# Regrouping the attention output through memory before normalising it, and a final projection in two fp32r products

## The reference, cut to what matters

```python
# xattn: softmax over 4096 keys, for every batch, head and query row
dot = einsum('bhsd,bhtd->bhst', Q, K) / 4
out = einsum('bhst,bhtd->bhsd', softmax(dot), V)
out = out.reshape(B, T_src, D_MODEL)     # [b,h,s,d] read as rows of 256, WITHOUT a transpose back
x = x + out @ Wh.T + bh
x = x + linear_attention(layernorm(x))   # features exp(..), causal A, ctx / max(den, 1e-6), @ Wout
x = x + ffn(layernorm(x))                # (silu(x@wg.T) * (x@wu.T)) @ wd.T, integer weights / 127
```

## Time and profile before

| | |
|---|---|
| median of three runs | 877.13 us |
| the profiled execution, whole | 875.48 us |
| its span, first to last instruction | 873.8 us |
| mean granted TensorE clock | 0.990 |
| main loop's last value product ends at | 796.9 us of the span |
| the last batch's tail, with nothing beside it | 796.9 to 873.8 us |

### The profile page before, as it was taken

The page is one execution under the profiler, slowest core; times in us unless marked ns, Lnnn a source line. Parts: engine busy times, 40 slices in busy tenths (PEclk is TensorE's granted clock), DMA queues, the critical chain, the costliest instruction groups (busy, mean ns, idle before and its releaser), DMA issues.

```text
span 873.8 us, 20543 instructions
## 1 busy us (share of the span) xinstructions
PE 829.1 (95%) x8817; PEld 569.8 (65%) x8817; DVE 417.2 (48%) x746; ACT 541.5 (62%) x598; POOL 47.1 (5%) x76
## 2 busy tenths in 40 slices
PE   6899999999999998999999998999999999989876
PEld 5666666666666666676666665667666666657656
DVE  7433236444644445534654446354474444402654
ACT  2478887776577665667567764575657666672141
POOL 1034000000000000000000000000000000000010
PEclk9899999999999999999999999999999999999999
DMA  7486654646344333346343441443614333202000
GB/s 248 172 258 237 241 183 166 209 158 193 122 146 146 142 125 133 122 133 191 136 146 145 146 142 53 158 158 129 195 65 170 122 122 119 100 2 50 0 2 15
DMA packets 58768, 120.08 MB, mean 137 GB/s; under 512 B 21552, under 2 KB 29744, under 8 KB 55152
## 3 DMA queue, kind: packets, MB, share of 16 engines
q1 hardware_dynamic: 56880, 114.31, 38.3%
q0 software_dynamic: 1792, 4.40, 1.7%
HBM read 78.84 MB, written 37.75 MB: 133 GB/s over the span
## 4 chain that ended last, share of the span: by engine, by line
PE 82%; DVE 8%; issue 4%; DMA 2%; ACT 2%; DVEq 1%; POOL 1%; SPq 0%; POOLq 0%; ACTq 0%
PE ps_o L816 26%; PE ps_s L828 18%; PE ps_pa L662 10%; PE ps_pa L617 10%; PE ps_pa L763 2%; PE ps_pa L692 2%; PE ps_pa L788 2%; PE ps_pa L775 2%; PE ps_pa L754 1%; ACT probs L1258 1%; PE ps_pa L740 1%; DMA oscr<-y 1%; PE ps_pa L684 1%; PE ps_pa L795 1%; PE ps_pa L767 1%
## 5 line engine op out<-in xcount | busy, mean ns | idle before, releaser
L1258 ACT ACTIVATE probs<-ps_s 128x1024 f32<-128x1024 f32 x512 | 496.8, 1023 | 234.2 <-PE ps_s L828 227.7
L816 PE MATMUL ps_o<-probs,values 128*17 128x256 f32 x4096 | 256.1, 385 | 0.0
L828 PEld LDWEIGHTS ps_s<-qstack,kstack 64*128 64x128 f32 x2048 | 140.0, 186 | 99.6 <-ACT probs L1258 48.8
L828 PE MATMUL ps_s<-qstack,kstack 64*128 64x256 f32 x2048 | 194.0, 307 | 5.3 <-ACT probs L1258 5.3
L816 PEld LDWEIGHTS ps_o<-probs,values 128*17 128x17 f32 x4096 | 104.1, 98 | 98.7 <-issue 9.8
L1343 DVE TENSOR_SCALAR kparts<-ps_pa,b_heads 128x512 fp32r<-128x512 f32 x64 | 48.0, 750 | 107.4 <-PE ps_pa L617 107.1
L662 PE MATMUL ps_pa<-wv_hi,ctx_hi 128*128 128x256 f32 x256 | 79.6, 311 | 2.9 <-DVE wv_lo L1331 2.2
L1360 DVE TENSOR_TENSOR values<-ps_pa,bv_pair 128x512 f32<-128x512 f32 x64 | 44.2, 690 | 77.5 <-PE ps_pa L662 77.1
L662 PE MATMUL ps_pa<-wv_lo,ctx_hi 128*128 128x256 f32 x256 | 72.5, 283 | 0.0
L662 PE MATMUL ps_pa<-wv_hi,ctx_lo 128*128 128x256 f32 x256 | 72.4, 283 | 0.0
L617 PE MATMUL ps_pa<-ctx_hi,wk_hi 128*128 128x512 f32 x128 | 56.4, 441 | 0.0
(11 more groups left out here) (274 smaller groups left out, 786.7 us busy)
## 6 DMA issues: line engine op xcount, KB each, us to landing
kstack<-kscr SPq DMA_DIRECT2D x96, 512.0 KB, 5.3
kscr<-kparts SPq DMA_DIRECT2D x64, 512.0 KB, 2.7
ctx_raw<-ctxT SPq DMA_DIRECT2D x32, 512.0 KB, 6.5
qstack<-qscr SPq DMA_DIRECT2D x12, 256.0 KB, 3.5
qscr<-qparts SPq DMA_DIRECT2D x4, 512.0 KB, 3.1
xh<-x SPq DMA_DIRECT2D x4, 256.0 KB, 5.4
kstack<-kstack SPq DMA_DIRECT2D x2, 512.0 KB, 6.0
qstack<-ksample SPq DMA_DIRECT2D x4, 256.0 KB, 3.6
```

The lines of the kernel that those rows point to most:

```text
L816: last = mm(ps_o[32 * j:32 * j + DH + 1, g * S:(g + 1) * S], values[par][:, i, head_of_step(g, j), :], prob[:, j * S:(j + 1) * S], start=b ...
L828: last = mm(ps_s[s % 2][:, j * S:(j + 1) * S], kstack[par][rows, u, i * P:(i + 1) * P], queries[rows, u, :], start=True, stop=True)
L1258: nc.scalar.activation(probs[n % AHEAD][:, :], ps_s[n % 2][:, :], ACT.Exp, scale=float(DH) ** -0.5).then_inc(fast["exp_done"], 1)
```

## The change

1. **Loop, output's way.** `oT0` and `oT1` are gone. After `o`, SyncE writes `o_sb` as it is (heads on partitions, not normalised, denominators and unused rows too) to `oscr` in four DMAs of 32 partitions, pieces of 1 KB, 512 KB in all. Then it reads it back in two DMAs whose pieces are 64 B, to `o_rows`, which lies in the buffer `feat`: 128 rows x 17 x 16 for each half. A new VectorE stage `on` at step 9 waits for that read, takes all reciprocals in one instruction, checks all denominators at once, and scales with one instruction for each half into `y`. `yT` at 12 now waits for VectorE, not for a DMA.
2. **Loop, norms.** The addition of the `wh` and `wout` products is a stage by itself and the layernorm behind it another one, `ln1`, `ln2`, at the same step.
3. **Weights of the down projection.** They are loaded as integers to `qk` and `y` in two DMAs and cast once, at set-up, to an fp32r array `wd_r`. The loop multiplies by the same array read as fp32.
4. **The end, output's way.** As in 1; two of the four writes are issued by SyncE and two by ScalarE. The transposes of `o_sb` go, 34 `warm` products stand in one place where 12 and 26 stood, the denominator check stands behind the copy of `yT0`, and the verdict behind the first layernorm.
5. **The end, down.** VectorE cuts each `hid[:, k, :]` in a high and a low fp32r part (two more instructions and two waits for its own pipe for each k), and TensorE makes two fp32r products for each k and half, where one full fp32 product stood.

```diff
-AT = {"o": 1, "oT0": 3, "oT1": 4, "yT": 12, "wh": 13, "ln1T": 19, ...
+AT = {"o": 1, "on": 9, "yT": 12, "wh": 13, "ln1": 13, "ln1T": 19, ...
...
-        oscr = scratch("oscr", [H, S, DH], FP32)
+        oscr = scratch("oscr", [ST, 2 * DH, HALF, S], FP32)
+        o_rows = feat_flat[:, 0:ST * (DH + 1) * DH].rearrange("p (t d u) -> p t d u", t=ST, d=DH + 1)
...
+        def write_heads(eng, c, j):
+            t, e = j // CI, j % CI
+            eng.dma_start(oscr[t].rearrange("d (g e) s -> e d g s", e=CI)[e],
+                          o_sb[32 * j:32 * j + 2 * DH, :, :]).then_inc(c["o_written"], 16)
...
             def write_output(c, clock):
-                wait_all((c["operand"], c.at("operand", clock, "oT1")))
+                wait_all((c["operand"], c.at("operand", clock, "o")))
+                for j in range(GH):
+                    write_heads(sp, c, j)
+            def read_rows(t, landed):
+                sp.dma_start(o_rows[:, t, :, :], oscr[t, 0:DH + 1].rearrange("d h (a u) -> (h a) d u", u=DH)).then_inc(landed, 16)
             def regroup_output(c, tails):
-                wait_all((c["o_written"], tails * 32 + 32))
+                wait_all((c["o_written"], tails * (16 * GH) + 16 * GH))
                 for t in range(ST):
-                    sp.dma_start(oscr[:, t * P:(t + 1) * P, :].rearrange("h s d -> s h d"), ...
+                    read_rows(t, c["o_in"])
...
                 elif name == "yT":
-                    pe.wait_ge(c["o_in"], clock[1] * 16 + 16)
                     last = transpose_blocks(bank, y)
...
-                    last = mm((ps_p, ps_a)[t][:, 0:D], hid[:, k, t * P:(t + 1) * P], wd_sb[:, k, :],
-                              start=k == 0, stop=k == HB - 1)
+                    for part in range(2):
+                        last = mm((ps_p, ps_a)[t][:, 0:D], last_part(k, part)[:, t * P:(t + 1) * P], wd_r[:, k, :],
+                                  start=k + part == 0, stop=k + part == HB)
...
+            warm(ps_p, 34)
             for t in range(ST):
-                pe.wait_ge(*vector_of("o0"))
-                ... (transposes of o_sb, warm(12), the judged transpose, warm(26), waits for the DMAs)
+                pe.wait_ge(*vector_of(f"y{t}"))
+                turn_rows(halves[2 + t], t, y).then_inc(last_product, 1)
...
+                elif name == "on":
+                    dve.wait_ge(c["o_in"], clock[1] * (16 * ST) + 16 * ST)
+                    if c is fast and tails:
+                        dve.wait_ge(c["stored"], tails * 16)
+                    v.reciprocal(rden[:, :, :], o_rows[:, :, DH, :])
+                    check_rows()
+                    for t in range(ST):
+                        last = scaled_rows(t)
...
+            def scaled_rows(t):
+                return v.tensor_tensor(y[:, t, :].rearrange("p (u d) -> p d u", d=DH), o_rows[:, t, 0:DH, :],
+                                       rden[:, t, :].unsqueeze(1).to_broadcast([P, DH, DH]), ALU.mult)
+            def check_rows():     # on [P, 2, 32] at once: tensor_scalar, tensor_tensor, tensor_reduce, tensor_tensor
...
-                v.scalar_tensor_tensor(hid[:, k, :], gate_e[:, k % 2, :], 1.0, hid[:, k, :], ALU.add, ALU.mult
-                                       ).then_inc(last_vector, 1)
+                v.scalar_tensor_tensor(hid[:, k, :], gate_e[:, k % 2, :], 1.0, hid[:, k, :], ALU.add, ALU.mult)
+                dve.drain()
+                if k >= HALF // 2:
+                    dve.wait_ge(*product_of(f"gu{HB - 1}"))
+                cut(last_part(k, 0), last_part(k, 1), hid[:, k, :]).then_inc(last_vector, 1)
```

More of the change, by code:

```diff
@@ L68 @@
          8: ("v", 0, 0), 10: ("v", 1, 0), 12: ("v", 2, 0), 13: ("v", 3, 0)}
-VECTOR_ONLY = ("ln0", "kbd0", "kbd1", "qcopy", "qcopy0", "fullmax", "o", "ss0", "ss1", "norm0", "norm1",
+VECTOR_ONLY = ("ln0", "ln1", "ln2", "kbd0", "kbd1", "qcopy", "qcopy0", "fullmax", "o", "on", "ss0", "ss1", "norm0", "norm1",
                *(f"gate{k}" for k in range(HB)))
@@ L86 @@
            "max3": 116, "maxT": 118}
-LAST_PRODUCTS = ["oT0", "oT1", "yT0", "yT1", "wh0", "wh1", "ln1T0", "ln1T1", "qk0", "qk1", "v", "qkT0", "qkT1",
+LAST_PRODUCTS = ["yT0", "yT1", "wh0", "wh1", "ln1T0", "ln1T1", "qk0", "qk1", "v", "qkT0", "qkT1",
                  "feat0", "feat1", "A0", "A1", "feat2", "pv0", "A2", "A3", "feat3", "pv1", "A4", "A5", "pv2", "A6", "A7", "pv3",
@@ L134, in __init__ @@
             "operand": (head, TAIL),
-            "powered": (["ln0"], ["wh", "wout"]),
+            "powered": (["ln0"], ["ln1", "ln2"]),
             "acted": ([], FEATS + GATES), "kfeat": ([], FEATS),
@@ L1178, in _ @@
             pool.wait_ge(fast["k_stacked"][1], 3 * STACKED)
-            pool.dma_start(wd_sb[:, :, :].bitcast(INT32), wr(wdT)).then_inc(i_in, 16)
+            for k, part in zip((0, HB - CI), wd_int):
+                n = part.shape[1]
+                pool.dma_start(part, wr(wdT)[:, k:k + n, :]).then_inc(i_in, 16)
             def weighted(c, f, clock):
@@ L1190, in stage @@
                     weighted(c, FEATS.index(name), clock)
-                elif name in ("ln0", "wh", "wout"):
+                elif name in ("ln0", "ln1", "ln2"):
                     power(c, name, clock)
@@ L1286, in _ @@
                                  ).then_inc(last_scalar, 1)
+            act.wait_ge(*vector_of("o0"))
+            act.wait_ge(*scalar_of("o1"))
+            for j in range(CI, GH):
+                write_heads(act, fast, j)
             last_columns("yT1", "yT1", halves[3])
@@ L1412, in normalise @@
-                by_half = bank[:, :].rearrange("p (g a e c) -> p a g e c", a=CI, e=CI, c=32)
-                scale = rden[:, :].rearrange("p (g a e) -> p a g e", a=CI, e=CI)
-                for a in range(CI):
-                    last = v.tensor_tensor(y[:, t, a * P:(a + 1) * P].rearrange("p (g e d) -> p g e d", e=CI, d=DH),
-                                           by_half[:, a, :, :, 0:DH],
-                                           scale[:, a, :, :].unsqueeze(3).to_broadcast([P, G, CI, DH]), ALU.mult)
@@ L1418, in normalise @@
-                return last
+                heads, scale = bank[:, :].rearrange("p (h c) -> p h c", c=32), rden[:, t, :]
+                v.tensor_scalar(scale, heads[:, :, DH], floor, None, ALU.max)
+                dve.drain()
+                v.reciprocal(scale, scale)
+                dve.drain()
+                return v.tensor_tensor(y[:, t, :].rearrange("p (h d) -> p h d", d=DH), heads[:, :, 0:DH],
+                                       scale.unsqueeze(2).to_broadcast([P, H, DH]), ALU.mult)
@@ L1514, in stage @@
                 elif name in ("wh", "wout"):
-                    v.tensor_tensor(xs[:, :, :], xs[:, :, :], bank[:, :].rearrange("p (t d) -> p t d", t=ST), ALU.add)
-                    dve.drain()
+                    last = v.tensor_tensor(xs[:, :, :], xs[:, :, :], bank[:, :].rearrange("p (t d) -> p t d", t=ST), ALU.add)
+                elif name in ("ln1", "ln2"):
                     last = layernorm(c, name, clock)
@@ L1624, in setup_tail @@
                     v.tensor_copy(wu_r[:, k, :], wu_int[k])
-                v.tensor_copy(wd_sb[:, :, :], wd_sb[:, :, :].bitcast(INT32))
+                for k, part in zip((0, HB - CI), wd_int):
+                    v.tensor_copy(wd_r[:, k:k + part.shape[1], :], part)
                 dve.drain()
```

135 lines of the change are left out of this document (45 added, 90 removed), and 2 rows, old and new, of the table AT.

## The result

The changed kernel takes 887.19 us (median of four runs, 885.03 to 889.71) against 877.81 us for the kernel before in the same comparison: 1.0099 times the time, interval 1.0063 to 1.0136. It is slower, as forecast, by 9.4 us where I said 4.5, and inside the range of 875.3 to 888. The profiled execution is the fastest of the four: 885.03 us, span 883.3 us, mean granted clock 0.981 where before had 0.990.

The account below looks back on a forecast made before the run. The prediction took TensorE, busy 95% of the span, as the bound. It summed loop +4.6, casts +0.1, end's output way -2.2 and down +2.0 to +4.5 us: 881.6 us, range 875.3 to 888 (own range 878.5 to 885).

Parts of the forecast that it names:

- the transposes' 3.8 us: Loop, TensorE: removing `oT0` and `oT1` gains 1.26 us a batch, 3.8 us for three batches.
- the end's two terms: After the loop: output's way gains 2.2 us, the down products in two fp32r parts lose 2.0 us.
- Writes landed, 6.7 us: Loop, SyncE's queue: from the first possible write issue to all four writes landed, 6.7 us, bounds 4.4 and 7.5.
- Reads landed, 4.5 us: Loop: the reads back in 64 B pieces take 4.5 us, bounds 3.5 and 5.5.
- The rival by which 64 B reads cost 3.8 us more than writes: Loop and end: 64 B reads fetch extra units of their line, +3.8 us in four places, 896.8 us; chance 0.05.
- `on`, 2.3 us: Loop, VectorE: reciprocal, checks, two scalings and the drain take 2.3 us, bounds 1.9 and 2.7.
- x: Loop: time from SyncE's first possible write issue to the end of `on`, 13.5 us; the loop's change is zero at 12.0.
- The clock: Rival, loop: clock falls at TensorE's new waits; 884.6 us for one, 887.6 for two, 890.6 for three; chance 0.15.
- Norms apart, 0: Loop: separating `ln1`, `ln2` from the additions costs nothing, as the next product after the released bank is six steps later.
- The end, output's way, -2.2: After the loop: `wh` starts 2.5 us earlier, the verdict costs 0.3; together -2.2 us, bounds -3.5 and -0.5.
- Down, +2.0: The end: a cast and a subtraction on VectorE for each k cost 2.0 us, bounds -0.8 and +4.6.
- Casts, 0.1: Set-up: two casts for one and one more DMA for the integer weights cost 0.1 us.

Follow-up runs that it names:

- run 6: Changed kernel with SyncE's output writes, their wait and the reads ahead of `kstack` and the load of `xs`: 871.22 us, 0.9918 of the kernel before.
- run 3: Changed kernel with 16 products that nobody reads on TensorE ahead of its wait at `yT` in the loop: 880.44 us, 1.005 of the kernel before.
- run 1: Changed kernel with the output's stages from `on` to `qkT` all four steps later: 891.55 us, 1.0185 of the kernel before.
- run 5: Kernel before with only the norms set apart from the additions of the `wh` and `wout` products: 873.69 us, 0.9939 of the kernel before.
- run 10: Kernel of run 7 with the norms `ln1` and `ln2` joined again to `wh` and `wout`: 871.80 us, 0.9944 of the kernel before.
- run 4: Changed kernel with the end's down back to one full fp32 product, no cut on VectorE: 884.44 us, 1.0078 of the kernel before.
- run 8: Changed kernel with the output's steps four places later and a projection between those otherwise back to back: 875.83 us, 0.9964 of the kernel before.
- run 2: Changed kernel with SyncE's four output writes ahead of `kstack` and `xs`, the reads in their old place: 885.69 us, 1.0106 of the kernel before.
- run 7: Changed kernel with the edits of run 6 and run 4 together: 867.08 us, 0.9863 of the kernel before.
- run 9: Kernel of run 7 with `on` one step earlier, at 8 for 9: 867.40 us, 0.9899 of the kernel before.

## Why the prediction was right, and where it was wrong

The mechanism and the sign were right: the wait moves from the DMA to VectorE's `y`, the transposes' 3.8 us don't pay for it, the end's two terms cancel. The number is partly luck: 887.19 us is outside the forecast's own 878.5 to 885, and inside the whole range because two things that I had not counted run against each other. From my +4.5 us it is +2.4 at the wait, +7.7 by the clock, -4.2 where norms are apart, -1.7 at before's late fall and +0.9 in the start-up: +9.6, and the profiled spans differ by 9.5. By its steps:

- *Writes landed, 6.7 us*: 7.7. The median of one such write from issue to landing was 5.5 us, and 2.6 in run 6, where nothing stood before them. My upper bound was 7.5.
- *Reads landed, 4.5 us*: 5.06, 4.70 and 5.04. Bounds held. Whether memory confirms a read sooner than a write, my reason for 4.5, no run tests. The rival by which 64 B reads cost 3.8 us more than writes did not come: with an empty queue before them (run 6) one read of 136 KB landed 3.4 us after its issue, median.
- *`on`, 2.3 us*: 2.25 (the two scalings 1.02 for my 0.85, the rest shorter).
- So x was 15.0, 14.6 and 14.9 for 13.5, and the wait 12.0 for 9.6. This is the mis-sized term of the sum: +2.4 us. It scatters: in run 3, with the same queue, x was 13.8, 14.2 and 14.7.
- *The clock* was a rival at 0.15 and happened in full. I called three falls 9 us; they were 7.1 to 7.7. It should not have been a rival beside the forecast but part of it: my own waits of 3 us were the condition (and more than was needed, run 1 has falls behind 1.76 us), and the trace of before already had a fall behind a wait of 2.68 us in the loop, at 542 us, which I had not looked for. A row of the stretch 544 to 548 would have been worth more than that of the start-up.
- *Norms apart, 0*: this is the step that failed outright. "The next product is six steps later" looked at `wh` only; behind `wout` the next head stage's transposition wants the bank at once. Run 5 has 6.1 us for the part by the medians, run 10 4.4, their traces 4.2 and 2.9, in both mostly the clock.
- *The two errors nearly met.* In the ledger the three entries came to 14.7 us for my 4.6, and 5.9 us that nobody had promised came back: -0.3 and -3.9 with norms apart, -1.7 where before's clock was low at 780 us. That last fall is nothing that the change removed, as far as the traces show. All traces have a wait of 1.74 to 1.76 us between 757 and 782 us, at a gate product that waits for `amat`; right behind it the clock falls in runs 3, 4, 5 and 8 and stays at 1.00 in the changed kernel and in runs 1, 2, 6, 7, 9 and 10. In the kernel before it falls at 781 us, 16 us behind that wait and after none longer than 0.9 us. Why in the one execution and not in the other stays open.
- *The end, output's way, -2.2*: -1.9 at `wh` (I had -2.5 there), -2.15 at the feed-forward. *Down, +2.0*: +2.1; cast 0.29 and subtraction 0.42 for my 0.25 and 0.40. *Casts, 0.1*: the difference to before grows by 0.09 us between 131 and 151 us, where they stand.

Is regrouping through memory with 32-row writes bad, then? No: runs 5 and 7, of one comparison, differ by the regrouping (in the turned order, loop and end, with the cut weights) and not by the norms or the end's down, and run 7 is 6.6 us faster. Not all of that is the regrouping's own: by the traces the loop's three entries give 1.8 us of it and the way to `wh` at the end 1.6, while run 5's trace has two late falls of the clock that run 7's has not. What made the change a loss was its place in the queue behind transfers nobody was in a hurry for, and the clock behind that.

## What to carry to other kernels

Before a round trip through memory is put into a pipeline, sort its queue by who waits: a write and a read that something waits for at once, behind 1.8 MB of loads with slack, cost here 9.5 us of waiting and 7 to 8 of clock, and turning the order brought the ratio to before from 1.0099 to 0.9918, some 16 us. Price a wait on TensorE of 1.7 us or more with the clock behind it, and look in the trace of before for falls that are there already: they are gains that an innocent edit may collect. And ask of a bank that is held through a normalisation who the very next user is, at every place where the code is shared.

## What the runs showed of the hardware

- The granted clock fell behind each of the nine waits of TensorE for `y` in the changed kernel and in runs 2 and 4, 3.2 to 4.8 us long. Behind waits of 2.0 to 2.7 us it fell in four of seven: 2.31 us yes and 2.32 us no in run 10, 2.33 us no and 2.68 us yes in the kernel before, 2.06 us yes twice and 2.35 us no in run 1. Behind waits of 1.74 to 1.76 us in the loop it fell in seven of fifteen, the row below, of run 3, among them. So a shorter wait is no safe one. One fall cost 1.7 us (before's at 781 us) to about 3 (before's at 542 us).

```profile
766.96 0.38 PE L796 MATMUL ps_pa<-x_hi,wg 128*128 128x256 f32 x1 [1.74 <-DVE amat L1580]
```

- Products whose result is thrown away kept it at 1.00 through a delay of nearly the same length (run 3).
- A write of 128 KB landed 5.5 us after issue (median of the changed kernel's) where most stood behind three 512 KB reads and one of 256 KB in the queue, 2.6 us in run 6 without them. Reads in 64 B pieces, two of 136 KB, had landed 5.06 us after the first issue, in run 9 4.2 to 4.4 us; in one microsecond of that (the changed kernel's stretch below) the DMA engines were 0.94 busy at 87 GB/s:

```profile
210.00:211.00 1.00, 0.12 (x2) 0.00 (x0) 0.00 (x0) 1.00 (x2) 0.00 (x0) 1.00 0.94 87
```

- Four such writes held SyncE's queue for 3.34 us at issue, 0.84 each, and the context load behind the reads 2.18 us, where the load of `xs` held it 0.58: issue is not the same price everywhere in this queue.
